# A last stage in which VectorE scales every tile and GpSimd only gathers

## The chip, the cores and the metric

One core of a Trainium2 chip runs the kernel. The time is what the device takes for one execution, in microseconds (us). Three runs of the kernel before gave 1338.32, 1339.25 and 1347.78 us; the median is 1339.25 us.

## The reference

A graph with 10,000 nodes (rows of 512 float32) and 5,000 edges goes through two layers, and each layer ends in a LayerNorm over the 512 columns of a row:

```python
x = _layernorm(x + _L0_gnn_ref(x, W, b, edge_index))      # graph convolution
x = _layernorm(x + _L1_gnn_ref(x, edge_attr, src, dst, ...))  # attention over the edges

# the end of _L1_gnn_ref:
out = segment_sum(m, dst, num_segments=n) ; out = out @ Wo.T + bo
out = node_feat + out
mean = out.mean(axis=0) ; var = jnp.mean(jnp.square(out - mean), axis=0)
out = (out - mean) * rsqrt(var + EPS) * gamma + beta
```

What matters here is the very end. After the attention each node row is `x + u`, where `u` is a message that only nodes with an incoming edge have. A normalisation by column (over all nodes) turns it into `(x + u) * scale + shift`, with one scale and one shift for each of the 512 columns. Then the row `x` is added once more and the LayerNorm by row follows.

## The kernel before

The rows are in 79 tiles of 128 nodes by 512 columns. The stages run one after the other: sorting of the edges, layer 0 over the node tiles, the attention over 20 blocks of 256 edges, and the last stage, `finish_stage`, which all of this case is about. It starts when the sums by column are complete (L2044 and what follows turns them into scale and shift) and then passes over the 79 tiles once. For tile j:

- **ScalarE** copies `x1(j)` (loaded by SyncE's queue, four tiles to a transfer) into the buffer `u(j)` (L2000). There are 12 such buffers; the copy of tile j waits until tile j-12 is summed.
- **GpSimd** then issues an indirect DMA, "the gather" below (L1945), which overwrites those rows of `u(j)` that have a message with their row of `msg_table`. So `u(j)` holds x + u.
- The **scaling** multiplies `u(j)` by the row of scales. For three tiles in four VectorE does it (L2083), reads `u(j)` from SBUF and the scale row from PSUM (`scale = ps[1]`), and writes into one of seven PSUM banks. For tiles with `j % 4 == 2` (`by_pool`) GpSimd does it (L1952) in place in SBUF, with a copy of the scale row in SBUF (`scale_row`), four places behind its gathers (`LATE = 4`).
- **TensorE** adds shift and x1 in the bank: two products for tiles that VectorE scaled (L1992, L1993), three for the others (L1984, L1985, L1987), where the scaled row has to be brought into PSUM too. So that VectorE's own writes can be added to, each bank is first written whole once (`write_whole`, L1956).
- **VectorE** takes the row statistics (`bn_stats`, L2093) and their aggregate (`bn_aggr`, L2100), and for each pair of tiles a reciprocal (L2089) and a bias (L2096); **ScalarE** takes the square root for a pair (L2025) and the normalising pass `y = bank * rstd + bias` (L2030); **SyncE** stores y (L1931, 8 buffers).

The order on each engine is written out by hand, with lags in tiles. VectorE's iteration k is: scaling of k, reciprocal of the pair k-4 (`PAIRED`), statistics of k-2 (`STATS`), bias of that pair, aggregate of k-2. The aggregate waits until the statistics just in front of it are written (`wait_alone`). The scaling of k waits for its gather and until the normalising pass that last read its bank, that of tile k-7, is done (`norm_ok`). ScalarE's iteration k is: copy of k, root of the pair k-12 (in every second iteration), normalising pass of k-15; that pass waits for the pair's bias and until the store that last used its y buffer has landed.

Of the kernel before, what the change touches and what calls it, by code (L numbers as in the profile page):

```python
# [25 lines left out]
ALU = mybir.AluOpType  # L26
# [9 lines left out]
NT = -(-N // P)  # L36
NP = NT * P
ET = -(-E // P)
EP = ET * P
# [15 lines left out]
def wait(eng, sem, count):  # L55

    if isinstance(count, int) and count <= 0:
        return
    eng.wait_ge(sem, count)  # L59


def wait_alone(eng, sem, count, passed):


    eng.wait_ge(sem, count)
    eng.sem_inc(passed, 1)  # L66
# [201 lines left out]
def prologue_stage(nc, g):  # L268
# [6 lines left out]
    PRE = 11  # L275
    LATE = 4
    with ExitStack() as ctx:
# [1547 lines left out]
def finish_stage(nc, g):  # L1825


    sb, sem = g.sb, g.sem
    R = 12
    RY = 8  # L1830
    RM = 8
    AHEAD = 10
    PAIR, NORM = 12, 15
    STATS, PAIRED = 2, 4
    LATE = 4
    with ExitStack() as ctx:
        more = sb(ctx, "fin_x1_more", [P, HOMES - 8, K * D])
        consts = sb(ctx, "fin_consts", [P, 3, K])
        mean = sb(ctx, "fin_mean", [P, K])
        var = sb(ctx, "fin_var", [P, K])  # L1840
        factor = sb(ctx, "fin_factor", [P, 2, K])
        hi = sb(ctx, "fin_factor_hi", [P, 2, K], F32R)
        lo = sb(ctx, "fin_factor_lo", [P, 2, K])
        lo_turned = sb(ctx, "fin_shift_lo_turned", [P, K])
        mirror = sb(ctx, "fin_mirror", [P, P])
        scale_hi = sb(ctx, "fin_scale_hi", [P, K, P], F32R)
        scale_lo = sb(ctx, "fin_scale_lo", [P, K, P], F32R)
        shift_hi = sb(ctx, "fin_shift_hi", [P, K, P])
        shift = sb(ctx, "fin_shift", [P, K, P], F32R)
        ones_r = sb(ctx, "fin_ones", [P, P], F32R)  # L1850
        scale_row = sb(ctx, "fin_scale_row", [P, D])
        stats = sb(ctx, "fin_stats", [P, RM, 6])
        mv = sb(ctx, "fin_mv", [P, RM, 2])
        root = sb(ctx, "fin_root", [P, RM, 1])
        rstd = sb(ctx, "fin_rstd", [P, RM, 1])
        bias = sb(ctx, "fin_bias", [P, RM, 1])
        u_more = sb(ctx, "fin_u_more", [P, K * D])
        ps = g.ps
        g.x1_homes = g.x1_homes + [more[:, i, :] for i in range(HOMES - 8)]
        scale = ps[1]  # L1860
        sum_banks = ps[3:8] + [ps[0], ps[2]]

        def quarter(slot, j):
            return slot[:, j % 4 * D:(j % 4 + 1) * D]

        def x1(j):
            return quarter(g.x1_homes[j // 4 % HOMES], j)

        def u(j):
            return quarter((g.over_lo[:, WK, :], g.over_lo[:, WV, :], u_more)[j // 4 % 3], j)  # L1870

        def y(j):
            return quarter((g.over_lo, g.over_hi)[j // 4 % 2][:, WO, :], j)

        def bank(j):
            return sum_banks[j % 7][:]

        def by_pool(j):
            return j % 4 == 2

        def scaled_by_pool(j):
            return sum(by_pool(i) for i in range(j + 1))

        def scaled_in_psum(j):
            return j + 1 - scaled_by_pool(j)

        const_in = g.const_in
        sums_ok = g.sums_ok
        u_ok, tot_ok, var_ok, std_ok, mirrored = (sem(n) for n in (
            "fin_x_copied", "fin_totals", "fin_var_ok", "fin_std", "fin_mirrored"))  # L1890
        split_ok, rows_ok, wide_ok, shift_ok = (sem(n) for n in (
            "fin_factors_split", "fin_rows_spread", "fin_scale_spread", "fin_shift_ok"))

        u_in = g.sum_in + g.x_in[2:4] + g.part_in + g.x_in[0:2] + g.again_in
        x_in = g.node_in + g.x1_out
        x_before = [landed(NT - 1 - s, 0, 0, 8) for s in range(8)] + [landed(NT - 1 - s, 0, 0, 4) for s in range(4)]
        u_before = [landed(NT - 1 - s, 0, 0, 4) for s in range(4)] + [32 * ET // 4] * 2 + [32 * NB // 2] * 2 + [32 * ET // 4 + 16] * 2 + [16 * (NB - 2)] * 2
        us_ok, pool_ok, sum_ok, stat_ok, root_ok, scale_ok, norm_ok = (sem(n) for n in (
            "fin_u_scaled_in_psum", "fin_u_scaled_by_pool", "fin_y_summed", "fin_stat", "fin_root_ok", "fin_scale_ok", "fin_norm"))
        open_ok = g.open_ok  # L1900
        BANKS = 4 + len(sum_banks)
        SCALE_IN_PSUM, SCALE_ROW = 1, 2
        y_out = g.w_in[1:5] + g.row_out[0:2] + g.u_out
        y_before = [32] * 3 + [16] + [16 * ET // 4] * 2 + [16 * NB] * 2
        mine = g.step_v
# [30 lines left out]
    def gpsimd_program(pool):  # L1936
        pool.wait_ge(g.coef_scanned, K * (NB - 1))
        nc.gpsimd.affine_select(out=mirror[:], in_=g.ones[:], compare_op=ALU.is_equal, fill=0.0, base=1 - P, pattern=[[1, P]], channel_multiplier=1).then_inc(mirrored, 1)
        for out in g.u_out:
            pool.wait_ge(out, 16 * NB)  # L1940

        for k in range(NT + LATE):
            if k < NT:
                pool.wait_ge(u_ok, k + 1)
                nc.gpsimd.indirect_dma_start(out=u(k), out_offset=None, in_=g.msg_table,  # L1945
                                             in_offset=bass.IndirectOffsetOnAxis(ap=g.last_edge[:, k:k + 1], axis=0),
                                             bounds_check=EP - 1, oob_is_err=False).then_inc(u_in[k % R], 16)
            j = k - LATE
            if j >= 0 and by_pool(j):
                pool.wait_ge(wide_ok, SCALE_ROW)  # L1950
                pool.wait_ge(u_in[j % R], u_before[j % R] + 16 * (j // R + 1))
                nc.gpsimd.tensor_tensor(u(j), u(j), scale_row[:], ALU.mult).then_inc(pool_ok, 1)  # L1952

    def tensor_program(pe):
        def write_whole(to):
            pe.matmul(to[:], g.w(g.w_hi, WO, 0, 0, P), g.w(g.w_hi, WO, 0), start=True, stop=True).then_inc(open_ok, 1)  # L1956
# [18 lines left out]
        pe.wait_ge(split_ok, 6)  # L1975
        for whole in sum_banks[5:7]:
            write_whole(whole)
        pe.wait_ge(shift_ok, K)

        for j in range(NT):  # L1980
            if by_pool(j):
                wait(pe, norm_ok, j - 6)
                pe.wait_ge(u_ok, j + 1)
                pe.matmul(bank(j), ones_r[:], shift[:].rearrange("p k n -> p (k n)"), start=True, stop=False)  # L1984
                pe.matmul(bank(j), g.ident[:], x1(j), start=False, stop=False)  # L1985
                pe.wait_ge(pool_ok, scaled_by_pool(j))
                pe.matmul(bank(j), g.ident[:], u(j), start=False, stop=True).then_inc(sum_ok, 1)  # L1987
            else:

                pe.wait_ge(u_ok, j + 1)  # L1990
                pe.wait_ge(us_ok, scaled_in_psum(j))
                pe.matmul(bank(j), ones_r[:], shift[:].rearrange("p k n -> p (k n)"), start=False, stop=False, skip_group_check=True)  # L1992
                pe.matmul(bank(j), g.ident[:], x1(j), start=False, stop=True, skip_group_check=True).then_inc(sum_ok, 1)  # L1993

    def scalar_program(act):
        def copy(j):
# [35 lines left out]
    def vector_program(dve):  # L2032
        v = nc.vector
# [42 lines left out]

        dve.wait_ge(open_ok, BANKS)
        for k in range(NT + PAIRED + 1):
            j = k
            if j < NT and not by_pool(j):  # L2080
                dve.wait_ge(u_in[j % R], u_before[j % R] + 16 * (j // R + 1))
                wait(dve, norm_ok, j - 6)
                v.tensor_tensor(bank(j), u(j), scale[:], ALU.mult).then_inc(us_ok, 1)  # L2083
            done = k - PAIRED
            pair = 0 <= done < NT and (done % 2 == 1 or done == NT - 1)
            m, n = done // 2 * 2 % RM, done % 2 + 1
            if pair:
                dve.wait_ge(root_ok, done // 2 + 1)
                v.reciprocal(rstd[:, m:m + n, :], root[:, m:m + n, :]).then_inc(scale_ok, 1)  # L2089
            j = k - STATS  # L2090
            if 0 <= j < NT:
                dve.wait_ge(sum_ok, j + 1)
                v.bn_stats(stats[:, j % RM, :], bank(j)).then_inc(stat_ok, 1)  # L2093
            if pair:
                dve.wait_ge(scale_ok, done // 2 * 2 + 1)
                v.scalar_tensor_tensor(bias[:, m:m + n, :], mv[:, m:m + n, 0:1], -1.0, rstd[:, m:m + n, :], ALU.mult, ALU.mult).then_inc(scale_ok, 1)  # L2096
            if 0 <= j < NT:
                wait(dve, norm_ok, j - RM + 1)
                wait_alone(dve, stat_ok, 2 * j + 1, g.passed)
                v.bn_aggr(mv[:, j % RM, :], stats[:, j % RM, :]).then_inc(stat_ok, 1)  # L2100

    return sync_program, scalar_program, gpsimd_program, tensor_program, vector_program

# [36 lines left out]
```

## Time and profile before

| | us |
|---|---|
| median of three runs | 1339.25 |
| profiled execution | 1341.85 |
| its span | 1339.9 |
| busy over the span: TensorE / VectorE / ScalarE / GpSimd | 1278.4 / 1081.9 / 636.7 / 815.9 |

The span is the time from the first to the last instruction in the trace; the execution's own time lies 1.95 us above it. The passes of the last stage over its tiles start at 1208.30 us of the span. The rows quoted further down are of three kinds. A row of a timeline is one instruction or a short run of one kind ("x2"): start, duration from the first start to the last end, engine, line, operation, what it writes and reads, and at the end in brackets how long the engine had been idle, and what ended that. The step from one start to the next start on the same engine is what an instruction costs, as durations overlap a little. A row of windows gives the busy time of each engine in one stretch.

### The profile page before, as it was taken

What the parts mean: (1) busy time and instruction counts of PE and PEld (TensorE: products, weight loads), DVE (VectorE), ACT (ScalarE), POOL (GpSimd) and SP (SyncE); (2) the same over time, 40 slices, a digit from 0 to 9 for tenths busy, and PEclk for the clock granted to TensorE, in tenths of its full rate; (3) what the DMA queues carried; (4) which work ended last, traced back from release to release, by engine and by line L of the source; (5) the groups of instructions that cost most, each with busy time, mean ns of one, the idle gap of its engine ahead of it and who ended that gap; (6) DMA issues with size and microseconds to landing.
All of it is one profiled execution on the core that took longest, in us unless ns stands there. A gap on an engine that the chain in (4) does not pass through costs nothing. (4 is left out here: it accounts for less than half of the span.)

```text
span 1339.9 us, 21776 instructions
## 1 busy us (share of the span) xinstructions
PE 1278.4 (95%) x6374; PEld 1028.6 (77%) x6374; DVE 1081.9 (81%) x2035; ACT 636.7 (48%) x1243; POOL 815.9 (61%) x752
## 2 busy tenths in 40 slices
PE   7899999999999699999999999999999999979997
PEld 5778878888888588888888888888888888754332
DVE  7577569999998226888888988888888888888897
ACT  3577547888887212333223323322332333257886
POOL 3667256677675443556666656566666565568885
PEclk9999999999999799999999999999999999879999
DMA  8889768787885514544444344444445443759986
GB/s 282 288 288 309 267 217 274 258 273 260 258 261 172 173 48 111 142 143 137 112 112 131 123 125 130 138 141 130 137 142 142 142 142 95 231 175 385 292 293 222
DMA packets 128300, 257.95 MB, mean 193 GB/s; under 512 B 21459, under 2 KB 21907, under 8 KB 128114
## 3 DMA queue, kind: packets, MB, share of 16 engines
q1 hardware_dynamic: 97490, 175.31, 39.9%
q0 software_dynamic: 29920, 80.38, 20.5%
q10 hardware_dynamic: 832, 1.57, 0.4%
q8 instruction: 26, 0.43, 0.1%
q14 instruction: 32, 0.26, 0.1%
HBM read 197.18 MB, written 73.60 MB: 202 GB/s over the span
## 5 line engine op out<-in xcount | busy, mean ns | idle before, releaser
L208 PE MATMUL ps<-w_lo,w_hi 128*128 128x512 f32 (+2 forms) x1140 | 416.4, 365 | 3.9 <-DVE w_lo L1432 1.4
L210 PE MATMUL ps<-w_hi 128*128 128x512 f32 (+2 forms) x1140 | 410.5, 360 | 0.0
L209 PE MATMUL ps<-w_hi,w_lo 128*128 128x512 f32 (+2 forms) x1140 | 410.4, 360 | 0.0
L208 PEld LDWEIGHTS ps<-w_lo,w_hi 128*128 128x128 f32 x1140 | 217.5, 191 | 36.5 <-DVE w_lo L1514 1.9
L210 PEld LDWEIGHTS ps<-w_hi 128*128 128x128 f32 x1140 | 217.2, 191 | 32.4
L209 PEld LDWEIGHTS ps<-w_hi,w_lo 128*128 128x128 f32 x1140 | 217.6, 191 | 29.6
L1270 POOL TENSOR_TENSOR acc_x<-acc_x,node_rows 128x512 f32<-128x512 f32 x72 | 114.9, 1595 | 86.2 <-DMA node_rows<-x_table 81.9
L925 POOL TENSOR_TENSOR node_y<-node_z,node_x 128x512 f32<-128x512 f32 x79 | 102.6, 1299 | 72.2 <-issue 34.0
L208 PE MATMUL ps<-w_lo,agg_hi 128*128 128x512 f32 x316 | 131.5, 416 | 1.2 <-DVE agg_lo L994 1.2
L209 PE MATMUL ps<-w_hi,agg_lo 128*128 128x512 f32 x316 | 124.8, 395 | 0.0
L210 PE MATMUL ps<-w_hi,agg_hi 128*128 128x512 f32 x316 | 124.7, 395 | 0.0
L1472 DVE TENSOR_TENSOR_SCAN v_turned<-coef_all,carry,v_turned 128x256 f32<-128x256 f32 x76 | 107.7, 1473 | 0.7
L1230 POOL DMA_INDIRECT edge_rows<-x_table,edge_gather_idx x72 | 80.2, 1114 | 42.2 <-POOL edge_gather_idx L1226 28.5
L1361 ACT CAST w_hi<-v_turned 128x1024 fp32r<-128x1024 f32 x17 | 17.9, 1051 | 157.3 <-DVE v_turned L1472 157.3
L1496 DVE TENSOR_TENSOR k_rows<-ps,bk_row 128x512 f32<-128x512 f32 x40 | 27.5, 690 | 73.1 <-PE ps L210 73.1
L929 POOL DMA_INDIRECT node_sum<-sum_table,last_edge x75 | 72.6, 968 | 16.6 <-DVE node_agg L1023 5.2
L1384 ACT ACTIVATE v_turned<-ps,bv_col 128x256 f32<-128x256 f32 x76 | 29.8, 474 | 94.8 <-PE ps L210 94.8
L945 ACT COPY node_z<-ps 128x512 f32<-128x512 f32 x79 | 46.3, 587 | 52.6 <-PE ps L210 52.6
L712 DVE TENSOR_TENSOR_SCAN node_x<-goes_on,node_x,ps 128x128 f32<-128x128 bf16 x156 | 62.0, 462 | 10.6 <-PE ps L624 10.6
L1253 POOL TENSOR_TENSOR k_rows<-k_rows,q_rows 128x512 f32<-128x512 f32 x38 | 49.2, 1296 | 35.0 <-DVE k_rows L1496 34.6
L210 PEld LDWEIGHTS ps<-w_hi,agg_hi 128*128 128x128 f32 x316 | 59.3, 188 | 14.5
L208 PE MATMUL ps<-w_lo,ea_hi 128*128 128x512 f32 x160 | 67.0, 419 | 3.4 <-DVE ea_lo L704 3.4
(279 smaller groups left out, 2866.0 us busy)
## 6 DMA issues: line engine op xcount, KB each, us to landing
node_x<-in_x SPq DMA_DIRECT2D x79, 256.0 KB, 4.1
x_table<-node_x SPq DMA_DIRECT2D x79, 256.0 KB, 2.2
node_rows<-x_table SPq DMA_DIRECT2D x79, 256.0 KB, 8.4
coef_all<-coef_table SPq DMA_DIRECT2D x38, 512.0 KB, 7.3
edge_part<-part SPq DMA_DIRECT2D x40, 256.0 KB, 4.4
out_dram<-rows_over_w_lo SPq DMA_DIRECT2D x40, 256.0 KB, 6.3
node_x<-in_ea SPq DMA_DIRECT2D x38, 256.0 KB, 4.8
msg_table<-dst_rows_and_msg SPq DMA_DIRECT2D x38, 256.0 KB, 5.1
```

Of the source, the lines that this page charges most:

```text
L208: pe.matmul(to, left[0], right[1], start=first, stop=False, skip_group_check=onto)
L209: pe.matmul(to, left[1], right[0], start=False, stop=False, skip_group_check=onto)
L210: return pe.matmul(to, left[0], right[0], start=False, stop=last, skip_group_check=onto)
L712: v.tensor_tensor_scan(run[:, t % R, k, :], g.goes_on[:, t * P:(t + 1) * P], ps_x[t % 2][:, k * P:(k + 1) * P], before, ALU.mult, ALU.add) ...
L925: nc.gpsimd.tensor_tensor(y[:, i % RY, :], z[:, i % 2, :], xr[:, i % RX, :], ALU.add).then_inc(y_ok, 1)
L929: nc.gpsimd.indirect_dma_start(out=rn[:, t % RS, :], out_offset=None, in_=g.sum_table, in_offset=bass.IndirectOffsetOnAxis(ap=g.last_edge[ ...
L945: nc.scalar.copy(z[:, q, :], ps_o[(s - 6) % 4][:]).then_inc(z_ok, 1)
L1230: nc.gpsimd.indirect_dma_start(out=rows[:, q, o, :], out_offset=None, in_=g.x1_table, in_offset=bass.IndirectOffsetOnAxis(ap=at, axis=0)). ...
L1253: nc.gpsimd.tensor_tensor(k_rows[:, q, :], k_rows[:, q, :], q_rows[:, q, :], ALU.mult).then_inc(qk_ok, 1)
L1270: nc.gpsimd.tensor_tensor(g.acc_x[r, :], g.acc_x[r, :], node[r, q, :], ALU.add).then_inc(x_added, 1)
L1384: nc.scalar.activation(vt[:, (s - 1) % 2, m, :], two(ps_r)[m // 2][:, m % 2, :], ACT.Identity, bias=g.bv_col[:, m:m + 1]).then_inc(v_ok, 1)
L1472: v.tensor_tensor_scan(vt[:, s, m, :], coef[:, m, 0, :], vt[:, s, m, :], carry[:, m:m + 1], ALU.mult, ALU.add).then_inc(scan_ok, 1)
```

## The change

VectorE scales all 79 tiles; GpSimd's queue holds the 79 gathers and nothing else. The scale row is read from its copy in SBUF, and the PSUM bank in which it stood becomes the eighth bank for sums (it is written whole as the last one, after ScalarE has copied the row out). TensorE has two products for every tile. VectorE's iteration k is now: statistics of k-3, reciprocal of the pair k-5, scaling of k, bias, aggregate of k-3; the scaling waits for the normalising pass of tile k-8. The core of the diff:

```diff
-    STATS, PAIRED = 2, 4
-    LATE = 4
+    STATS, PAIRED = 3, 5
...
-        sum_banks = ps[3:8] + [ps[0], ps[2]]
+        sum_banks = ps[3:8] + [ps[0], ps[2], scale]
...
-        for k in range(NT + LATE):
-            if k < NT:
-                pool.wait_ge(u_ok, k + 1)
...
-            j = k - LATE
-            if j >= 0 and by_pool(j):
-                pool.wait_ge(wide_ok, SCALE_ROW)
-                pool.wait_ge(u_in[j % R], u_before[j % R] + 16 * (j // R + 1))
-                nc.gpsimd.tensor_tensor(u(j), u(j), scale_row[:], ALU.mult).then_inc(pool_ok, 1)
+        for k in range(NT):
+            pool.wait_ge(u_ok, k + 1)
...
+        pe.wait_ge(wide_ok, SCALE_ROW)
+        write_whole(scale)
         pe.wait_ge(shift_ok, K)
...
-            if by_pool(j):
-                wait(pe, norm_ok, j - 6)
...
+            pe.wait_ge(u_ok, j + 1)
+            pe.wait_ge(us_ok, j + 1)
...
         for k in range(NT + PAIRED + 1):
-            j = k
-            if j < NT and not by_pool(j):
-                dve.wait_ge(u_in[j % R], u_before[j % R] + 16 * (j // R + 1))
-                wait(dve, norm_ok, j - 6)
-                v.tensor_tensor(bank(j), u(j), scale[:], ALU.mult).then_inc(us_ok, 1)
-            done = k - PAIRED
+            stat, done = k - STATS, k - PAIRED
             pair = 0 <= done < NT and (done % 2 == 1 or done == NT - 1)
             m, n = done // 2 * 2 % RM, done % 2 + 1
+            if 0 <= stat < NT:
+                dve.wait_ge(sum_ok, stat + 1)
+                v.bn_stats(stats[:, stat % RM, :], bank(stat)).then_inc(stat_ok, 1)
             if pair:
                 dve.wait_ge(root_ok, done // 2 + 1)
                 v.reciprocal(rstd[:, m:m + n, :], root[:, m:m + n, :]).then_inc(scale_ok, 1)
-            j = k - STATS
-            if 0 <= j < NT:
-                dve.wait_ge(sum_ok, j + 1)
-                v.bn_stats(stats[:, j % RM, :], bank(j)).then_inc(stat_ok, 1)
+            if k < NT:
+                dve.wait_ge(u_in[k % R], u_before[k % R] + 16 * (k // R + 1))
+                wait(dve, norm_ok, k - len(sum_banks) + 1)
+                v.tensor_tensor(bank(k), u(k), scale_row[:], ALU.mult).then_inc(us_ok, 1)
```

Bias and aggregate follow as before, with `stat` in the place of `j`.

## Rows read from the trace of the kernel before

**Rows 1.** Windows: a stretch of 20 us in the last stage, by engine.
```profile
core 0: us, PE busy (x) PEld busy (x) DVE busy (x) ACT busy (x) POOL busy (x), PEclk, DMA share, GB/s
1280.00:1300.00 20.00, 18.30 (x46) 7.87 (x45) 18.07 (x48) 16.17 (x32) 16.54 (x17) 1.00 0.85 274
```

**Rows 2.** Timeline of GpSimd, from one gather to the fourth after it.
```profile
1275.46 0.99 POOL L1945 DMA_INDIRECT rows_over_w_lo<-msg_table,last_edge  x1 [0.31 <-issue]
1276.76 1.00 POOL L1945 DMA_INDIRECT rows_over_w_lo<-msg_table,last_edge  x1 [0.30 <-issue]
...
1279.07 1.29 POOL L1952 TENSOR_TENSOR fin_u_more<-fin_u_more,fin_scale_row 128x512 f32<-128x512 f32 x1
...
1281.86 1.00 POOL L1945 DMA_INDIRECT rows_over_w_lo<-msg_table,last_edge  x1 [0.30 <-issue]
```

**Rows 3.** Timeline of VectorE over the same four tiles.
```profile
1275.31 0.70 DVE L2083 TENSOR_TENSOR ps<-rows_over_w_lo,ps 128x512 f32<-128x512 f32 x1 [0.34 <-DMA rows_over_w_lo<-msg_table,last_edge]
1275.91 0.16 DVE L2089 RECIPROCAL fin_rstd<-fin_root 128x2 f32<-128x2 f32 x1
1275.99 0.68 DVE L2093 BATCH_NORM_STATS2 fin_stats<-ps 128x6 f32<-128x512 f32 x1
1276.59 0.14 DVE L2096 SCALAR_TENSOR_TENSOR fin_bias<-fin_mv,fin_rstd 128x2 f32<-128x2 f32 x1
1276.80 0.18 DVE L2100 BATCH_NORM_AGGREGATE fin_mv<-fin_stats 128x2 f32<-128x6 f32 x1
1276.91 0.69 DVE L2083 TENSOR_TENSOR ps<-fin_u_more,ps 128x512 f32<-128x512 f32 x1
1277.52 0.69 DVE L2093 BATCH_NORM_STATS2 fin_stats<-ps 128x6 f32<-128x512 f32 x1
1278.34 0.18 DVE L2100 BATCH_NORM_AGGREGATE fin_mv<-fin_stats 128x2 f32<-128x6 f32 x1
...
1279.72 0.67 DVE L2096 SCALAR_TENSOR_TENSOR fin_bias<-fin_mv,fin_rstd 128x2 f32<-128x2 f32 x1
...
1281.59 0.70 DVE L2083 TENSOR_TENSOR ps<-fin_u_more,ps 128x512 f32<-128x512 f32 x1 [0.21 <-ACT rows_over_w_lo L2030]
```

**Rows 4.** Timeline of VectorE in the attention stage: operations with two SBUF inputs.
```profile
909.96 3.06 DVE L1579 TENSOR_TENSOR acc_xx<-acc_xx,node_rows 128x512 f32<-128x512 f32 x4
...
1159.67 1.27 DVE L1634 TENSOR_TENSOR k_rows<-k_rows,q_rows 128x512 f32<-128x512 f32 x2
```

**Rows 5.** Timeline where the last stage begins: VectorE, TensorE and the first statistics.
```profile
1206.99 1.22 PE L1956 MATMUL ps<-w_hi 128*128 128x512 f32 x2 [0.26 <-DVE fin_shift_lo_turned L2070]
...
1208.30 1.29 DVE L2083 TENSOR_TENSOR ps<-rows_over_w_lo,ps 128x512 f32<-128x512 f32 x2 [0.19 <-issue]
...
1211.65 0.70 DVE L2093 BATCH_NORM_STATS2 fin_stats<-ps 128x6 f32<-128x512 f32 x1 [2.06 <-PE ps L1993]
```

**Rows 6.** Timeline near the end: the statistics of the last tile.
```profile
1333.77 0.70 DVE L2093 BATCH_NORM_STATS2 fin_stats<-ps 128x6 f32<-128x512 f32 x1 [0.62 <-PE ps L1987]
```

**Rows 7.** Timeline of ScalarE: most of a pair of tiles without a wait.
```profile
1289.71 0.29 ACT L2025 ACTIVATE fin_root<-fin_mv,eps 128x2 f32<-128x2 f32 x1
1289.91 0.76 ACT L2030 ACTIVATE rows_over_w_hi<-ps,fin_bias,fin_rstd 128x512 f32<-128x512 f32 x1
1290.57 0.60 ACT L2000 COPY rows_over_w_lo<-rows_over_w_lo 128x512 f32<-128x512 f32 x1
1291.08 0.78 ACT L2030 ACTIVATE rows_over_w_hi<-ps,fin_bias,fin_rstd 128x512 f32<-128x512 f32 x1
```

**Rows 8.** DMA issues from 1215 to 1335 us (median us to landing last), and L1931.
```profile
rows_over_w_lo<-msg_table,last_edge POOLq DMA_INDIRECT x47, 5.4
...
DMA to landing us min/median/max: 1.6/4.9/9.0
```

**Rows 9.** Timeline at the first gather: a VectorE operation with two SBUF inputs.
```profile
1198.61 0.69 DVE L2044 TENSOR_TENSOR acc_xx<-acc_xx,sum_xx 128x512 f32<-128x512 f32 x1
1198.76 1.48 POOL L1945 DMA_INDIRECT rows_over_w_lo<-msg_table,last_edge  x1 [0.15 <-issue]
```

More of the change, by code:

```diff
@@ L1875, in bank @@
         def bank(j):
[L1876 to L1885, printed above, removed]
+            return sum_banks[j % len(sum_banks)][:]
         const_in = g.const_in
@@ L1897, in finish_stage @@
         u_before = [landed(NT - 1 - s, 0, 0, 4) for s in range(4)] + [32 * ET // 4] * 2 + [32 * NB // 2] * 2 + [32 * ET // 4 + 16] * 2 + [16 * (NB - 2)] * 2
-        us_ok, pool_ok, sum_ok, stat_ok, root_ok, scale_ok, norm_ok = (sem(n) for n in (
-            "fin_u_scaled_in_psum", "fin_u_scaled_by_pool", "fin_y_summed", "fin_stat", "fin_root_ok", "fin_scale_ok", "fin_norm"))
+        us_ok, sum_ok, stat_ok, root_ok, scale_ok, norm_ok = (sem(n) for n in (
+            "fin_u_scaled_in_psum", "fin_y_summed", "fin_stat", "fin_root_ok", "fin_scale_ok", "fin_norm"))
         open_ok = g.open_ok
@@ L1940, in gpsimd_program @@
             pool.wait_ge(out, 16 * NB)
-        for k in range(NT + LATE):
-            if k < NT:
-                pool.wait_ge(u_ok, k + 1)
-                nc.gpsimd.indirect_dma_start(out=u(k), out_offset=None, in_=g.msg_table,
-                                             in_offset=bass.IndirectOffsetOnAxis(ap=g.last_edge[:, k:k + 1], axis=0),
-                                             bounds_check=EP - 1, oob_is_err=False).then_inc(u_in[k % R], 16)
-            j = k - LATE
-            if j >= 0 and by_pool(j):
-                pool.wait_ge(wide_ok, SCALE_ROW)
-                pool.wait_ge(u_in[j % R], u_before[j % R] + 16 * (j // R + 1))
-                nc.gpsimd.tensor_tensor(u(j), u(j), scale_row[:], ALU.mult).then_inc(pool_ok, 1)
+        for k in range(NT):
+            pool.wait_ge(u_ok, k + 1)
+            nc.gpsimd.indirect_dma_start(out=u(k), out_offset=None, in_=g.msg_table,
+                                         in_offset=bass.IndirectOffsetOnAxis(ap=g.last_edge[:, k:k + 1], axis=0),
+                                         bounds_check=EP - 1, oob_is_err=False).then_inc(u_in[k % R], 16)
     def tensor_program(pe):
@@ L1977, in tensor_program @@
             write_whole(whole)
+        pe.wait_ge(wide_ok, SCALE_ROW)
+        write_whole(scale)
         pe.wait_ge(shift_ok, K)
         for j in range(NT):
-            if by_pool(j):
-                wait(pe, norm_ok, j - 6)
[L1983 to L1993, printed above, removed]
+            pe.wait_ge(u_ok, j + 1)
+            pe.wait_ge(us_ok, j + 1)
+            pe.matmul(bank(j), ones_r[:], shift[:].rearrange("p k n -> p (k n)"), start=False, stop=False, skip_group_check=True)
+            pe.matmul(bank(j), g.ident[:], x1(j), start=False, stop=True, skip_group_check=True).then_inc(sum_ok, 1)
     def scalar_program(act):
@@ L2096, in vector_program @@
                 v.scalar_tensor_tensor(bias[:, m:m + n, :], mv[:, m:m + n, 0:1], -1.0, rstd[:, m:m + n, :], ALU.mult, ALU.mult).then_inc(scale_ok, 1)
[L2097 to L2100, printed above, removed]
+            if 0 <= stat < NT:
+                wait(dve, norm_ok, stat - RM + 1)
+                wait_alone(dve, stat_ok, 2 * stat + 1, g.passed)
+                v.bn_aggr(mv[:, stat % RM, :], stats[:, stat % RM, :]).then_inc(stat_ok, 1)
     return sync_program, scalar_program, gpsimd_program, tensor_program, vector_program
```

## The prediction, made before the changed kernel was run

> **What bounds the kernel now.** I read the page first: only the last stage changes, so the row of windows for it comes next. No engine is full there: of 20 us VectorE is busy 18.07, TensorE 18.30, ScalarE 16.17, GpSimd 16.54, at a granted clock of 1.00 and a DMA share of 0.85 [rows 1]. So the timelines have to say who waits. GpSimd's queue does not: a gather starts every 1.30 us (1275.46 to 1276.76; it is busy 1.00 and the other 0.30 is its own issue), and its scaling of 1.29 us stands between two gathers. Four gathers and one scaling take 1281.86 - 1275.46 = 6.40 us, 1.60 us per tile, with no wait for anyone [rows 2]. VectorE covers the same four tiles in 1281.59 - 1275.31 = 6.28 us, with 0.34 us idle for a gather and 0.21 us idle for ScalarE [rows 3]. GpSimd sets the pace, and one place where it passes it on can be seen: the bias, two columns wide, takes 0.14 us at 1276.59 but 0.67 us at 1279.72, and ends at 1280.39, just after GpSimd's scaling, which ran from 1279.07 to 1280.36 [rows 2, 3]. The late aggregate then makes the root, the normalising pass and the next scaling late (the idle 0.21). From the first statistics at 1211.65 to those of the last tile at 1333.77 pass 122.12 us for 78 tiles, 1.57 each [rows 5, 6].
>
> **The change, part by part.** *GpSimd loses its 20 scalings.* Its queue then needs 1.30 us per tile instead of 1.60, and the waits of the bias go with them. It is no longer the bound if another engine needs more than 1.30.
>
> *VectorE gets those 20 scalings and a new order.* I rebuild its iteration from steps. Statistics to the next operation: 0.60 (1275.99 to 1276.59). Scaling to the next: 0.61 (1276.91 to 1277.52). Aggregate to the next: 0.11 (1276.80 to 1276.91). Today the aggregate comes 0.82 us after its statistics (1277.52 to 1278.34), as it must wait for them to be written; with the scaling between them, that wait of some 0.2 us is filled [rows 3]. A tile without pair work costs 0.60 + 0.61 + 0.11 = 1.32. Pair work adds the reciprocal, 0.08 (1275.91 to 1275.99), and the bias; its step to the aggregate, 0.21, is mostly the wait for the statistics, so it lies between 0.08 and 0.21 and I take 0.10, near the reciprocal of the same width. The pair costs 2 x 1.32 + 0.18 = 2.82: **1.41 us per tile**. At 0.21 it would be 1.465.
>
> *The scaling now reads both operands from SBUF.* No row shows this with a result in PSUM. The bounds: the product of two SBUF tiles at L1634 takes 1.27 us for two, a step of 0.60; the sum at L1579 takes 3.06 for four, a step of (3.06 - 0.69) / 3 = 0.79 [rows 4]. I take 0.61: L1579 adds into its own input, so that each waits for the one in front, and the scaling does not. The upper end would make the tile 1.59.
>
> *The eighth bank and the head.* TensorE writes one more bank whole before VectorE may start: half of the 1.22 us of the two written last, 0.61 [rows 5]. VectorE would do three scalings ahead of its first statistics instead of two, but these wait 2.06 us for TensorE today [rows 5], which covers the third (0.61). So the first statistics move to 1211.65 + 0.6 = 1212.25. They stand in iteration 3, so 76 full iterations follow (3 to 78), then two without a scaling before the last statistics: 0.82 + 0.11 each as today, and one pair, 0.18. Last statistics: 1212.25 + 76 x 1.41 + 1.86 + 0.18 = 1321.45, against 1333.77: **12.3 us earlier** [rows 5, 6]. What follows them (6.1 us to the end) has the same operations in the same order.
>
> *ScalarE.* It loses nothing and gains nothing. Root to pass 0.20, pass to copy 0.66, copy to pass 0.51, pass to copy 0.66, and the copy 0.60: 2.63 us per pair, 1.32 per tile [rows 7]. Against 1.41 it has 7% to spare. Its loop with VectorE: the scaling of an even k needs the pass of k-8, which follows the root that needs the aggregate of k-5. Aggregate start, root, end of pass and signal are 0.18 + 0.04 + 0.20 + 0.76 + 0.1, about 1.3 us; from that aggregate to the scaling VectorE has its own work of 0.11 + 1.32 + 0.60 + 0.08 = 2.11. So the wait that is 0.21 today falls away, with 0.8 to spare, thanks to the extra bank and the later place in the iteration.
>
> *TensorE.* It has 20 products fewer; 18.30 busy of 20 us at 12.5 tiles is 1.46 per tile now as the profile models it, but it stood idle for VectorE's scalings, and the statistics now come three iterations (4.2 us) after the scaling. I cost it at nothing. Its cover is the clock of 1.00 [rows 1]; at half of it a tile would cost more than 1.41.
>
> *Gathers and DMA.* A gather lands 5.4 us after its issue [rows 8]. ScalarE copies tile k about nine tiles ahead of VectorE's scaling of k (copy of k stands before the pass of k-15, and the passes follow the scalings by 6 to 7 tiles): 9 x 1.41 = 12.7 us less 1.3 of issue and 5.4 of landing leave 6. The same bytes move in less time: the share goes from 0.85 to 0.85 x 1.57 / 1.41 = 0.95 [rows 1]. The stores land within 9.0 us at most [rows 8], and the pass that reuses a buffer comes 8 x 1.41 = 11.3 us later, less its 0.76 and the issue: 1 us to spare at the worst. This is late next. Price of it: nothing below, up to 0.1 per tile above.
>
> *The lock between VectorE and GpSimd, now the other way round.* The first gather started 0.15 us after a VectorE addition of two SBUF tiles and took 1.48 us instead of 1.00 [rows 2, 9]; it seems to have been held until that addition ended. The new scaling is of that kind and runs 0.6 us of every 1.41. The bounds for a gather are 0 and 0.48. I take it to cost nothing, since a gather that is held leaves at the end of a scaling, and the next one is due 1.30 us later, at the end of the scaling after it: GpSimd falls into step with VectorE at 1.41 and no slower. The Trainium skill says the same of the cause: in "SBUF — State Buffer", section "Who interferes with whom", a VectorE instruction with two SBUF inputs contends with a GpSimd instruction that reads SBUF, and whoever comes first holds the shared port for its whole instruction. By that rule the waits of the bias go, as in the trace, but all 79 scalings now enter the contest, where today none of them does, and the sum would lie between the one above and the third rival below.
>
> **Sum.** 12.3 us off the profiled execution's 1341.85 gives 1329.5; off the median of 1339.25, 2.6 below that execution, it gives **1327.0**. About 1%, 13.4 us, is what a measurement of this kernel can tell from no change; the forecast falls just short of it.
>
> **The rivals.** *First, another engine or the DMA sets the pace* between 1.45 and 1.55: ScalarE waiting for stores, or gathers late under a share of 0.95 [rows 1, 8]. For it: two engines within 7% of VectorE and a DMA that is nearly full. Against it: today ScalarE waits for VectorE, and no DMA but one gather is waited for in these rows. At 1.50 the gain is 12.3 - 76 x 0.09 = 5.5: 1333.8 us.
>
> *Second, the scaling from two SBUF operands costs a step of 0.79* [rows 4], or the exchange does not pay in another way: the gain is 12.3 - 76 x 0.18 = -1.4: about 1340.6 us, no change. Against it: L1634.
>
> *Third, on the other side, the lock decides*: every gather is held by the whole 0.48 [rows 9] and GpSimd's step becomes 1.78, above the 1.60 of today. It decides from a mean hold of 0.30. The last gather would then start at 1198.76 + 1.78 x 78 = 1337.6; landing 5.4, scaling 0.7, TensorE about 1.5 and the 6.1 after the last statistics make a span of 1351.3, 11.4 more than now: 1350.7 us, and more if gathers land later. Against it stands the falling into step, which needs VectorE's regular beat.
>
> **Chances.** Forecast (pace 1.38 to 1.44, 1324.5 to 1329.5): 0.70. First rival (1330 to 1336): 0.15. Second (1337 to 1342): 0.07. Third, with a lower clock of TensorE, whose effect would have the same sign: 0.08. The limit of faster by over 1% is 1325.9. Of the forecast's range a bit over a third lies below it, at paces of 1.39 and less: faster 0.27. Slower by over 1% (above 1352.6) is most of the third case: 0.06. The rest, 0.67, is within 1%. The range of 8 in 10 takes the forecast and most of the first rival: 1324 to 1335 us.
>
> **What would show it.** In the profile after: scalings of VectorE 1.41 us apart on average, an aggregate about 0.6 us after its scaling starts, every bias near 0.14 us, gathers lengthened to at most 1.5 us and in step with VectorE, ScalarE's idle before the root down to about 0.2 us per pair, first statistics near 1212.3, last near 1321.5. Wrong would be: steps of the scaling well above 0.61 (second rival), gathers 1.6 us or more apart with VectorE waiting for DMA (third), a scaling that waits for ScalarE, or stores that land after 10 us (first).

## The result

The changed kernel takes 1323.56 us (median of four runs, 1319.59 to 1327.78), the kernel before 1340.40 (four runs, 1338.32 to 1347.78): the medians are 16.8 us apart. The ratio on record, 0.9858 with a 95% interval of 0.983 to 0.9885, stands for 19.0 us, 1.4% faster. The forecast was 1327.0 with a range of 1324 to 1335 and only 0.27 for faster by over 1%. It missed in size, not in sign.

The first lines of the page after the change (span, busy time by engine):

```profile
span 1317.9 us, 21697 instructions
PE 1265.1 (96%) x6335; PEld 1017.7 (77%) x6335; DVE 1076.7 (82%) x2055; ACT 636.2 (48%) x1243; POOL 790.8 (60%) x732
```

The profiled execution took 1319.59 us, 22.3 less than the one of before (1341.85); its span is 22.0 shorter. Not all of this belongs to the change. Where the last stage begins can be read from an instruction of GpSimd that both kernels have, in code that the change leaves alone. After:

```profile
1194.68 0.28 POOL L1928 TENSOR_SCALAR_AFFINE_SELECT fin_mirror<-ones 128x128 f32<-128x128 f32 x1
...
1208.44 0.70 DVE L2061 BATCH_NORM_STATS2 fin_stats<-ps 128x6 f32<-128x512 f32 x1 [1.45 <-PE ps L1970]
...
1311.72 0.67 DVE L2061 BATCH_NORM_STATS2 fin_stats<-ps 128x6 f32<-128x512 f32 x1
```

Before:

```profile
1198.31 0.30 POOL L1938 TENSOR_SCALAR_AFFINE_SELECT fin_mirror<-ones 128x128 f32<-128x128 f32 x1
```

It came 3.63 us earlier in this execution; over the profiles of this study it lies anywhere from 1194.3 to 1203.5, whatever the kernel. The rest is the stage's own, against [rows 5, 6]:

| stretch | before | after | difference |
|---|---|---|---|
| start to that instruction | 1198.31 | 1194.68 | -3.63 |
| from there to the first statistics | 13.34 | 13.76 | +0.42 |
| first to last statistics (78 tiles) | 122.12 | 103.28 | -18.84 |
| last statistics to the end | 6.13 | 6.18 | +0.05 |

So the stage gained 18.4 us, between the 16.8 of the medians and the 19.0 of the ratio, and all of it in the pace: 1.566 us per tile before, 1.324 after.

Windows of the stage after the change; columns as in [rows 1], whose row this answers:

```profile
1280.00:1300.00 20.00, 19.89 (x47) 7.30 (x45) 20.00 (x61) 19.32 (x38) 15.43 (x15) 1.00 0.98 342
```

VectorE went from 18.07 busy to 20.00 of 20 us: it is full, and ScalarE, at 19.32, nearly so. TensorE stands at 19.89, but its ends are modelled in the profile, and behind the first statistics VectorE waits for it nowhere. GpSimd has fallen from 16.54 to 15.43. The DMA share is 0.98. Timeline of VectorE, a little over two tiles:

```profile
1249.73 0.69 DVE L2061 BATCH_NORM_STATS2 fin_stats<-ps 128x6 f32<-128x512 f32 x1
1250.31 0.17 DVE L2064 RECIPROCAL fin_rstd<-fin_root 128x2 f32<-128x2 f32 x1
1250.38 0.70 DVE L2068 TENSOR_TENSOR ps<-fin_u_more,fin_scale_row 128x512 f32<-128x512 f32 x1
1250.97 0.18 DVE L2071 SCALAR_TENSOR_TENSOR fin_bias<-fin_mv,fin_rstd 128x2 f32<-128x2 f32 x1
1251.04 0.20 DVE L2075 BATCH_NORM_AGGREGATE fin_mv<-fin_stats 128x2 f32<-128x6 f32 x1
1251.13 0.69 DVE L2061 BATCH_NORM_STATS2 fin_stats<-ps 128x6 f32<-128x512 f32 x1
1251.71 0.71 DVE L2068 TENSOR_TENSOR ps<-fin_u_more,fin_scale_row 128x512 f32<-128x512 f32 x1
1252.30 0.20 DVE L2075 BATCH_NORM_AGGREGATE fin_mv<-fin_stats 128x2 f32<-128x6 f32 x1
1252.40 0.69 DVE L2061 BATCH_NORM_STATS2 fin_stats<-ps 128x6 f32<-128x512 f32 x1
```

No row has a bracket: VectorE waits for nobody. A pair of tiles takes 1252.40 - 1249.73 = 2.67 us. Against [rows 3], the 0.82 between statistics and aggregate is gone, and so are the idle 0.34 and 0.21; the bias is 0.18 us long here and 0.28 at most from 1225 to 1305 us, never 0.67. Timeline of GpSimd over the same time:

```profile
1249.70 1.01 POOL L1934 DMA_INDIRECT rows_over_w_lo<-msg_table,last_edge  x1 [0.30 <-issue]
1251.02 1.02 POOL L1934 DMA_INDIRECT rows_over_w_lo<-msg_table,last_edge  x1 [0.30 <-issue]
...
1253.65 1.05 POOL L1934 DMA_INDIRECT fin_u_more<-msg_table,last_edge  x1 [0.30 <-issue]
```

Gathers here follow each other at 1.31 to 1.35 us, where [rows 2] have a scaling between them. From 1249.70 to 1298.92 all of them but one begin 0.60 to 0.65 us behind the start of a scaling and take 1.00 to 1.05 us (the other began 0.37 behind it and took 1.29): GpSimd runs in step with VectorE. The fifth experiment shows what keeps it there. ScalarE, one pair:

```profile
1251.27 0.30 ACT L2002 ACTIVATE fin_root<-fin_mv,eps 128x2 f32<-128x2 f32 x1
1251.47 0.76 ACT L2007 ACTIVATE rows_over_w_hi<-ps,fin_bias,fin_rstd 128x512 f32<-128x512 f32 x1
1252.14 0.61 ACT L1977 COPY fin_u_more<-fin_x_more 128x512 f32<-128x512 f32 x1
1252.64 0.77 ACT L2007 ACTIVATE rows_over_w_hi<-ps,fin_bias,fin_rstd 128x512 f32<-128x512 f32 x1
1253.32 0.61 ACT L1977 COPY fin_u_more<-fin_x_more 128x512 f32<-128x512 f32 x1
1253.93 0.30 ACT L2002 ACTIVATE fin_root<-fin_mv,eps 128x2 f32<-128x2 f32 x1
```

From root to root 1253.93 - 1251.27 = 2.66 us, without a bracket either. It isn't full for all that: the copy in front of the root takes a step of 0.61 and the other one 0.50. In the kernel with half statistics below, where ScalarE hardly waits, both take 0.51 and the pair 2.55.

### The profile page after: what moved, and what is told of

It reads as the page before. It is cut to its first block and busy times, and to the rows that moved or that the text cites. A ratio compares the mean times of both kernels' runs of the same rounds, so it can differ in the third digit from the quotient of the medians.

```text
span 1317.9 us, 21697 instructions
## 1 busy us (share of the span) xinstructions
PE 1265.1 (96%) x6335; PEld 1017.7 (77%) x6335; DVE 1076.7 (82%) x2055; ACT 636.2 (48%) x1243; POOL 790.8 (60%) x732
## 3 DMA queue, kind: packets, MB, share of 16 engines
q10 hardware_dynamic: 832, 1.57, 0.4%
## 5 line engine op out<-in xcount | busy, mean ns | idle before, releaser
L1472 DVE TENSOR_TENSOR_SCAN v_turned<-coef_all,carry,v_turned 128x256 f32<-128x256 f32 x76 | 111.6, 1523 | 0.7
L1348 ACT CAST w_hi<-ps 128x512 fp32r<-128x512 f32 x40 | 21.5, 590 | 100.0 <-PE ps L1714 100.0
```

What stands on the lines that cost most here:

```text
L1472: v.tensor_tensor_scan(vt[:, s, m, :], coef[:, m, 0, :], vt[:, s, m, :], carry[:, m:m + 1], ALU.mult, ALU.add).then_inc(scan_ok, 1)
```

## The experiments

**Which part brings the gain.** Three parts can be taken separately: GpSimd's relief, the new order with its lags, and the eighth bank with the scale row in SBUF. First, the order alone, on the kernel before:

```diff
-    STATS, PAIRED = 2, 4
+    STATS, PAIRED = 3, 5
...
+            if 0 <= stat < NT:
+                v.bn_stats(...)          # ahead of the reciprocal
...
+            if k < NT and not by_pool(k):
+                v.tensor_tensor(bank(k), u(k), scale[:], ALU.mult)   # behind it
```

> The kernel before with the new order alone (statistics of k-3, scaling of k, aggregate of k-3); GpSimd still scales one tile in four, seven banks, scale row in PSUM. If GpSimd's queue (four gathers of 1.30 us and one scaling) sets the pace, the tile stays at 1.57 to 1.60 us and the time within 0.5% of before. If the wait between statistics and aggregate on VectorE was what counted, the pace falls by up to 0.2 us per tile and the time by up to 15 us.

Measured: ratio 1.0024 (1.0004 to 1.0044), 1.64 us per tile. The waits of VectorE from 1225 to 1305 us (total, times, longest):

```profile
DVE ps L2091 <- ACT rows_over_w_lo L2030: 6.8, 13, 0.5
DVE ps L2091 <- ACT rows_over_w_hi L2030: 6.3, 12, 0.9
```

The 0.2 us between statistics and aggregate is filled in the three tiles of four that VectorE scales, and a new wait takes its place: the scaling waits for the normalising pass that frees its bank, 13.1 us in some 49 tiles, 0.27 per tile. With statistics a tile later everything behind them comes a tile later, and seven banks are one too few. The expected pace of 1.57 to 1.60 was for GpSimd's queue as the limit. That limit is still there (four gathers and a scaling, 1.60 per tile [rows 2]), so the order alone could not have gained.

Second, GpSimd's relief alone, on the kernel before:

```diff
-            if j < NT and not by_pool(j):
+            if j < NT:
...
-                nc.gpsimd.tensor_tensor(u(j), u(j), scale_row[:], ALU.mult).then_inc(pool_ok, 1)
```

> The kernel before with VectorE scaling every tile and GpSimd only gathering; old order, seven banks, scale row in PSUM. From the steps of before: scaling 0.60, statistics to aggregate 0.82, aggregate 0.11, reciprocal 0.08 for a pair: 1.57 us per tile, as before; time within 0.5% of before. If GpSimd's relief alone made the gain, the tile takes 1.33 to 1.45 and the time falls by 10 to 19 us.

Measured: ratio 0.9977 (0.9963 to 0.999), 1.567 us per tile. A window of it:

```profile
1250.00:1270.00 20.00, 16.88 (x40) 6.16 (x39) 18.72 (x52) 17.09 (x33) 12.37 (x13) 1.00 0.88 285
```

GpSimd is down to 12.37 of 20 us, so it was relieved, but VectorE in the old order needs 1.57 by itself, the same as before. Two bounds lay one on the other. VectorE's row has 1.28 us of 20 that are not busy, and no DMA or other engine is the cause: they are the aggregate's wait for its own engine's statistics.

Third and fourth, the change with seven banks, the scale row in PSUM as before or in SBUF:

```diff
-        sum_banks = ps[3:8] + [ps[0], ps[2], scale]
+        sum_banks = ps[3:8] + [ps[0], ps[2]]
...
-                v.tensor_tensor(bank(k), u(k), scale_row[:], ALU.mult)
+                v.tensor_tensor(bank(k), u(k), scale[:], ALU.mult)      # p3 only
```

> The changed kernel with seven banks and the scale row in PSUM. The scaling of an odd k then waits for the normalising pass of k-7, which needs the aggregate of k-4 that stands 0.67 us in front of it and 1.29 us are needed: a wait of about 0.6 us per pair, 1.64 us per tile, some 5 us slower than before and 24 slower than the changed kernel. If the eighth bank does not matter: 1.33 and the time of the changed kernel. Theory A (VectorE's steps are 0.02 shorter when its queue is never held up) expects steps of 0.60 behind each wait and 0.58 elsewhere; theory B (the row in SBUF shortens the scaling) expects 0.60 to 0.61 for every scaling here.

> The changed kernel with seven banks, scale row in SBUF. Theory A: the same steps and time as with the row in PSUM (within 1 us). Theory B: scalings 0.02 us shorter than there, some 1.5 us less. If gathers and scalings hold each other up through the shared port, this one is slower than the one with the row in PSUM.

Measured: ratios 1.0017 (0.9998 to 1.0036) and 1.0012 (0.9993 to 1.0032), 1.616 us per tile in both. Where the scale row is read from makes no difference to the pace (0.005 us in the step of a scaling); the eighth bank is the whole difference between these two and the change. VectorE in the version with the row in PSUM:

```profile
1249.37 0.67 DVE L2059 BATCH_NORM_STATS2 fin_stats<-ps 128x6 f32<-128x512 f32 x1
1250.56 0.70 DVE L2066 TENSOR_TENSOR ps<-rows_over_w_lo,ps 128x512 f32<-128x512 f32 x1 [0.52 <-ACT rows_over_w_lo L2005]
1251.16 0.17 DVE L2073 BATCH_NORM_AGGREGATE fin_mv<-fin_stats 128x2 f32<-128x6 f32 x1
...
1251.90 0.68 DVE L2066 TENSOR_TENSOR ps<-rows_over_w_lo,ps 128x512 f32<-128x512 f32 x1
1252.48 0.16 DVE L2069 SCALAR_TENSOR_TENSOR fin_bias<-fin_mv,fin_rstd 128x2 f32<-128x2 f32 x1
```

The scaling at 1250.56 waited 0.52 us for ScalarE and takes a step of 0.60; the next one waited for nothing and takes 0.58. The two stand in different places, but in the change run again, where neither waits, those places differ by 0.005 only. This pair of rows bears on the miss, below.

Fifth, the change with the old order:

```diff
-    STATS, PAIRED = 3, 5
+    STATS, PAIRED = 2, 4
...             # scaling first, then reciprocal, statistics, bias, aggregate, as before
```

> The changed kernel (VectorE scales all, eight banks, scale row in SBUF) with the old order on VectorE: scaling, statistics of k-2, aggregate. If the order is what the gain needs, VectorE's wait between statistics and aggregate stays: 1.567 us per tile, the time of the kernel with VectorE scaling all and seven banks (0.998 of before). If the eighth bank brings the gain by itself: 1.33 to 1.45 per tile, 10 to 19 us below before.

Measured: ratio 1.0003 (0.998 to 1.0025), 1.567 us per tile. VectorE:

```profile
1251.28 0.70 DVE L2060 TENSOR_TENSOR ps<-rows_over_w_lo,fin_scale_row 128x512 f32<-128x512 f32 x1
1251.89 0.69 DVE L2070 BATCH_NORM_STATS2 fin_stats<-ps 128x6 f32<-128x512 f32 x1
1252.72 0.18 DVE L2077 BATCH_NORM_AGGREGATE fin_mv<-fin_stats 128x2 f32<-128x6 f32 x1
```

Statistics to aggregate is 0.83 again. Eight banks do nothing for a kernel that doesn't wait for a bank.

Beside the second experiment, which has the same order but the scale row in PSUM, this kernel also shows how a scaling with two SBUF inputs acts on a gather. A scaling and a gather of the second, then the gather that began 0.27 us behind the scaling at 1251.28 above:

```profile
1248.44 0.69 DVE L2058 TENSOR_TENSOR ps<-rows_over_w_lo,ps 128x512 f32<-128x512 f32 x1
1248.64 1.01 POOL L1934 DMA_INDIRECT rows_over_w_lo<-msg_table,last_edge  x1 [0.31 <-issue]
```

```profile
1251.55 1.30 POOL L1934 DMA_INDIRECT fin_u_more<-msg_table,last_edge  x1 [0.30 <-issue]
```

With the row in PSUM the gather begins 0.20 us behind the scaling and takes 1.01; with both operands in SBUF it takes 1.30. The 40 gathers of this kernel that begin less than 0.56 us behind a scaling's start all end 1.54 to 1.58 us behind that start, whenever they began; the 28 that begin later behind one take 1.00 to 1.01, and so do all 20 of the first kind in the second experiment. So a gather that begins under such a scaling is held until about 0.56 us of the scaling are over. It costs this kernel nothing, since GpSimd has room.

Sixth, the change with GpSimd still scaling one tile in four:

```diff
+            j = k - LATE
+            if j >= 0 and by_pool(j):
+                nc.gpsimd.tensor_tensor(u(j), u(j), scale_row[:], ALU.mult).then_inc(pool_ok, 1)
...
-            if k < NT:
+            if k < NT and not by_pool(k):
```

> New order, eight banks and scale row in SBUF, but GpSimd still scales one tile in four. If GpSimd's queue is a bound of its own, four gathers and one scaling keep the tile at 1.60 us or a little more (scalings of both engines with two SBUF inputs now stand in each other's way): time within 0.5% of before, or up to 8 us slower. If order and bank alone bring the gain: VectorE has three scalings in four, the tile falls to 1.33 or below and the time by 19 us.

Measured: ratio 1.0035 (1.0015 to 1.0056), 1.635 us per tile. VectorE, then GpSimd:

```profile
1249.52 0.66 DVE L2086 BATCH_NORM_STATS2 fin_stats<-ps 128x6 f32<-128x512 f32 x1
1250.10 2.42 DVE L2093 TENSOR_TENSOR ps<-rows_over_w_lo,fin_scale_row 128x512 f32<-128x512 f32 x1
1252.44 0.17 DVE L2100 BATCH_NORM_AGGREGATE fin_mv<-fin_stats 128x2 f32<-128x6 f32 x1
```

```profile
1249.66 1.00 POOL L1945 DMA_INDIRECT rows_over_w_lo<-msg_table,last_edge  x1 [0.30 <-ACT fin_u_more L2002]
1250.67 1.28 POOL L1952 TENSOR_TENSOR rows_over_w_lo<-rows_over_w_lo,fin_scale_row 128x512 f32<-128x512 f32 x1
1252.11 1.31 POOL L1945 DMA_INDIRECT rows_over_w_lo<-msg_table,last_edge  x1 [0.16 <-issue]
```

VectorE's scaling, 0.68 us elsewhere in this trace, takes 2.42 beside GpSimd's, and the gather behind takes 1.31 for 1.00. From 1225 to 1305 us GpSimd scales 12 times, and VectorE's scaling beside it lasts 2.42 to 2.45 us 11 times and 1.57 once; over the stage there are 18 such pairs, and in each VectorE's scaling ends 0.56 to 0.58 us after GpSimd's, whichever began first. With the row in PSUM (the first experiment) none is longer than 0.70; there the bias, whose inputs lie in SBUF too, is the one held (0.39 to 1.56 us). So this is the lock between scaling and scaling, once VectorE reads both operands from SBUF: 1.75 us per four tiles. It isn't what keeps this kernel from gaining, though. GpSimd's queue needs 1.60 per tile without any lock [rows 2], and the lock adds at most 0.07 to that (four tiles take 6.68 us here against 6.40). The parts of the change need each other: leaving out any one of the three (the third to sixth experiments) loses the gain, and no subset tried gained more than 0.3%.

**What the miss hangs on.** The change once more, and with the scaling first in the iteration again but the aggregate one tile later, so that it never waits for statistics just in front of it:

```diff
+            j = k                        # scaling of k, first in the iteration
...
+            j = k - 2                    # statistics of k-2
...
+            j = k - STATS                # aggregate of k-3, on a semaphore of its own
+                wait_alone(dve, stat_ok, j + 1, g.passed)
+                v.bn_aggr(mv[:, j % RM, :], stats[:, j % RM, :]).then_inc(aggr_ok, 1)
```

> The changed kernel with the scaling first again (scaling of k, reciprocal, statistics of k-2, bias), but with the aggregate one tile later (k-3), so that it never waits for the statistics in front of it. If what the new order saves is that wait, and VectorE's steps are 0.02 us shorter when nothing holds it up: steps of 0.58 to 0.59, 1.33 us per tile, the time of the changed kernel (0.986 of before). The scaling now stands 0.67 us earlier against ScalarE's pass, with some 0.1 us to spare, so that a few waits may make it 1.35. If the place of the scaling between statistics and aggregate matters in itself: 1.45 to 1.57.

> The changed kernel once more, beside the other two. 1.33 us per tile with every step as in its first trace (0.58 statistics, 0.59 scaling, 0.09 aggregate, 0.07 reciprocal and bias), whatever the stages ahead of it take; time 0.986 of before, within 0.002.

Measured: 0.9848 (0.9831 to 0.9864) and 0.9861 (0.984 to 0.9883), 1.334 and 1.333 us per tile. VectorE with the late aggregate:

```profile
1251.87 0.67 DVE L2061 TENSOR_TENSOR ps<-rows_over_w_lo,fin_scale_row 128x512 f32<-128x512 f32 x1
1252.45 0.69 DVE L2071 BATCH_NORM_STATS2 fin_stats<-ps 128x6 f32<-128x512 f32 x1
1253.05 0.17 DVE L2079 BATCH_NORM_AGGREGATE fin_mv<-fin_stats 128x2 f32<-128x6 f32 x1
1253.13 0.68 DVE L2061 TENSOR_TENSOR ps<-fin_u_more,fin_scale_row 128x512 f32<-128x512 f32 x1
```

Against the fifth experiment only the aggregate's place differs. Its hold is gone (0.83 to 0.60), and the step of the scaling went with it from 0.61 to 0.58, that of the aggregate from 0.11 to 0.08. The step of the statistics did not: with nothing held it is 0.60 (1252.45 to 1253.05), not the 0.58 to 0.59 that was expected. It is as fast as the change; the intervals overlap, so it doesn't beat it.

**What sets the pace now.** Each kernel halves the work of one engine per tile: the statistics, ScalarE's pass (from tile 8), both.

```diff
-                v.bn_stats(stats[:, stat % RM, :], bank(stat))
+                v.bn_stats(stats[:, stat % RM, :], bank(stat)[:, 0:D // 2])          # q1, q3
...
-                nc.scalar.activation(y(j), bank(j), ACT.Identity, ...)
+                w = D if j < RY else D // 2
+                nc.scalar.activation(y(j)[:, 0:w], bank(j)[:, 0:w], ACT.Identity, ...)   # q2, q3
```

> The changed kernel with row statistics over 256 of the 512 columns (left out: the other half), which takes 0.27 us per tile off VectorE (1.33 to 1.06). If ScalarE, whose pair takes 2.66 us as well, is a second bound: the pace stays at 1.33 and VectorE shows idle time behind ScalarE or GpSimd. If VectorE alone is the bound: 1.31, where GpSimd's gathers (1.30 to 1.31) stop it.

> The changed kernel with the normalising pass of ScalarE over 256 of the 512 columns from tile 8 on (left out: the other half of y), which takes 0.43 us per pair off ScalarE (2.66 to 2.23). If VectorE is a bound of its own: the pace stays at 1.33 and ScalarE idles 0.4 us per pair before the root. If only ScalarE was: 1.31.

> The changed kernel with row statistics and, from tile 8 on, the normalising pass over 256 of the 512 columns (left out: the other halves). VectorE needs 1.06 us per tile, ScalarE about 1.08. If GpSimd's gathers are the third bound: 1.31 us per tile as soon as their lead is used up, and VectorE waits for gathers. If the DMA (share 1.0) is: more than 1.31, with gathers or stores late.

Measured: ratios 0.984 (0.978 to 0.9899), 0.9858 (0.9798 to 0.9918) and 0.9847 (0.9827 to 0.9866); paces over the stage 1.284, 1.335 and 1.302. One window of each, in this order:

```profile
1250.00:1270.00 20.00, 19.67 (x48) 7.42 (x47) 18.27 (x64) 20.00 (x41) 15.43 (x16) 1.00 1.04 368
```

```profile
1250.00:1270.00 20.00, 19.87 (x46) 7.26 (x46) 20.00 (x62) 16.43 (x38) 15.43 (x16) 1.00 1.02 354
```

```profile
1230.00:1250.00 20.00, 17.73 (x47) 8.21 (x48) 17.04 (x64) 17.92 (x42) 15.73 (x15) 1.00 1.06 400
```

With a lighter ScalarE (16.43) nothing moves: VectorE stays at 20.00, so ScalarE's 19.3 to 19.9 of 20 was no second bound. With lighter statistics the pace improves by 0.04 to 0.05 only, then ScalarE is at 20.00. That pace is below the 1.31 expected from GpSimd's gathers, whose step is 1.345 there: they start 10 us ahead of the first scaling, and the stage ends before this lead is used up. With both lighter neither is full, and VectorE waits for gathers to land (total, times, longest, from 1208 to 1300 us):

```profile
DVE ps L2069 <- DMA rows_over_w_lo<-msg_table,last_edge: 9.4, 10, 3.4
```

One of its gathers, and the scaling under which it began:

```profile
1280.80 0.68 DVE L2069 TENSOR_TENSOR ps<-rows_over_w_lo,fin_scale_row 128x512 f32<-128x512 f32 x1
1280.96 1.40 POOL L1934 DMA_INDIRECT fin_u_more<-msg_table,last_edge  x1 [0.30 <-issue]
```

GpSimd is never idle here for more than the 0.30 of its own issue. Its gathers take 1.10 us on average, by the same hold as in the fifth experiment, and follow each other at 1.40 from the first to the last, while they land 6.2 us after their issue against 6.0 with half the pass alone (medians, rows_over_w_lo). So behind VectorE's 1.33 stand ScalarE at 1.28 and, with both out of the way, late gathers, mainly because GpSimd's full queue issues them at 1.40. Stores were late as well: ScalarE waited 2.8 us for two of them. That GpSimd's queue would be the bound in a longer stage is an estimate from these steps; no experiment took the holds away alone. Each pace of this group is that of one trace, and the times of the three can't be told from the change's. The DMA share alone doesn't tell whether gathers come late: the second of the three kernels had a window with nearly the same share and rate and VectorE full:

```profile
1230.00:1250.00 20.00, 19.84 (x46) 7.24 (x46) 20.00 (x60) 16.88 (x39) 15.43 (x16) 1.00 1.06 395
```

## Why the prediction was wrong

**The bound before: right, but half of it.** GpSimd at 1.60 per tile and the held bias [rows 2, 3] were as described; from first gather to last it made 1.59 per tile (the last began at 1322.95), and the stage ran at 1.57 out of the lead of its gathers. Taking GpSimd's scalings away alone gave 0.2%, since VectorE's old order, given all scalings, needs 1.567. The prediction had all three remedies in one sum, so this didn't hurt it.

**GpSimd's relief: right.** Its step is 1.31 (forecast 1.30), busy 15.43 of 20.

**The filled wait: right.** The aggregate starts 0.59 after its scaling (forecast 0.6) and waits for nothing.

**The eighth bank and ScalarE's loop: right.** No scaling waits for a bank; with seven banks each tile would lose 0.27 to 0.29. ScalarE had 4% to spare where 7% had been expected, because VectorE is faster than forecast. Its own need was put too high as well: the sum of 2.63 takes the last copy by its duration, 0.60, and not by its step, 0.51 [rows 7]; 2.55 was measured, 1.28 per tile.

**First statistics: right.** +0.42 from the stage's start (forecast +0.6). **The tail: right**, 6.18.

**The scaling's operands: right.** The row in SBUF or PSUM gave the same pace, 1.616. The second rival (a step of 0.79) did not occur.

**TensorE and the stores at nothing: right.** The clock granted is 1.00 in the window, nothing waited for TensorE once the stage ran, and ScalarE waited for two stores, 0.6 us in total. The latest store landed after 10.3 us (before 9.0), which the prediction had named as a sign of the first rival; the sign came without the slowdown.

**The lock with the gathers at nothing: right, and by the mechanism forecast.** A gather that begins under a scaling with two SBUF inputs is held until some 0.56 us of it are over (fifth experiment); the first gather of [rows 9] ended 1.63 us behind its addition's start, a little later than the 1.54 to 1.58 there. In the change GpSimd falls into step behind the scalings, as forecast, and the gathers take 1.03 us on average: a mean hold of 0.03, far from the 0.30 of the third rival, and below the 0.11 that would have put GpSimd's 1.30 above the forecast's 1.41. The lock between scaling and scaling cost VectorE 1.75 us per four tiles in the sixth experiment. The Trainium skill ("SBUF — State Buffer", section "Who interferes with whom") names this pair as contending, and the sixth experiment agrees. It also lets the first comer hold the port for its whole instruction; here VectorE's scaling began 0.57 us before GpSimd's and was the one lengthened, while GpSimd's kept its 1.28. The measurement decides: the one that starts first in the trace is not always the one that wins. The spans of GpSimd are rough in a profile, so when each engine asked for the port stays open.

**VectorE's pair: this step failed.** The prediction put it at 2 x (0.60 + 0.61 + 0.11) + 0.08 + 0.10 = 2.82 us, 1.41 per tile. Measured: 2 x (0.58 + 0.59 + 0.09) + 0.07 + 0.07 = 2.66, 1.33 per tile. Over 76 iterations that is 76 x 0.08 = 6.1 us; the forecast 12.3 and 6.1 make the 18.4 that the stage gained. The mechanism was right and its largest term mis-sized, by 0.02 or so in each instruction.

The difference of 0.16 per pair, from steps averaged over 80 us, is 0.04 in the two scalings, 0.04 in the two statistics, 0.04 in the two aggregates and 0.04 in reciprocal and bias. Where do they come from? The steps of [rows 3] were read in a queue that is held up once in every tile, by the aggregate's wait for the statistics in front of it. For the scaling and the aggregate this is the difference that counts. A scaling takes 0.60 to 0.61 behind a held aggregate (before, the second and fifth experiments) or when it has itself waited (the first, third and fourth), and 0.58 to 0.59 otherwise in these kernels and the change, whether it stands first or second in the iteration, and with the second operand in PSUM or SBUF. The late aggregate, against the fifth experiment, moves nothing else and shows both steps shrink.

The statistics do not follow this rule. They take 0.58 directly behind an aggregate, in the change and also in the first, third, fourth and sixth experiments, where other instructions are held. Behind a reciprocal they take 0.59 to 0.60 in the kernels with that hold, and the same with the late aggregate, which has none (0.60 behind the scaling there). So their share goes with the place that the new order gives them and not with the hold. Why an instruction after a hold takes longer to the next, and why the neighbour matters to the statistics, is not shown by any run.

The rows had a hint. The prediction bounded the scaling's step by L1634, "1.27 us for two, a step of 0.60" [rows 4]; less the 0.69 that it used for the other row of the group, this gives 0.58, the measured value. (The next operation starts 1.20 us behind the first of the two, so 0.60 is the mean of that step and of the one to the next operation.) The bias had bounds on both sides, 0.08 and 0.21; the scaling's lower end was that 0.60, and statistics and aggregate had no range at all. The bias came out at 0.07, below its lower bound.

**The chances.** The forecast lay 1 us from the limit of 1%, and its range ended 0.44 us above the measured median. That distance is less than the four runs differ among themselves, so on which side of 1324 the median fell was chance; the stage's own 18.4 us against 12.3 were not. There is also a slip in the working: of the forecast's range, 1324.5 to 1329.5, 1.4 of 5.0 us lie below 1325.9, 0.28 and not "a bit over a third", which makes 0.20 of the 0.27. With a bound from below on the steps (0.58 for the scaling, the same for the statistics of equal width, the reciprocal's 0.08 for the bias) the pair is 2 x (0.58 + 0.58 + 0.11) + 0.16 = 2.70 us and the gain 76 x 0.06 = 4.6 more, 1322.4: the range would have had to reach down to it, and "faster" deserved about half of the chance.

## What to carry to other kernels

When a sum is built from steps of one engine, take them from a stretch in which the engine isn't held up and the instruction has the neighbours that it will have, or give every term a bound from below as well: 0.02 us in 0.60, 76 times over a few instructions, was a third of the gain. Where an instruction waits for the one in front of it, work of another tile put between them fills the wait, but the deeper pipeline wants one more buffer; test both together, as each without the other showed nothing here. When two bounds coincide, neither remedy alone tells you anything about the pair.

## What the runs showed of the hardware

- VectorE's step for a scaling of 512 float32 columns is 0.58 to 0.59 us, and 0.60 to 0.61 after a hold; for statistics it is 0.58 behind an aggregate and 0.59 to 0.60 behind a scaling or a reciprocal. The change run again gives the same in another execution, 2.66 us for a pair:

```profile
1249.24 0.66 DVE L2061 BATCH_NORM_STATS2 fin_stats<-ps 128x6 f32<-128x512 f32 x1
...
1251.90 0.66 DVE L2061 BATCH_NORM_STATS2 fin_stats<-ps 128x6 f32<-128x512 f32 x1
```

- A scaling of VectorE with two SBUF inputs beside GpSimd's product takes 2.42 us for 0.68 and ends 0.56 to 0.58 us after it (18 of 18). Gathers do not lengthen it (0.81 at most, in a stretch of the change where every VectorE row reads some 0.1 us longer at unchanged steps).
- It does lengthen a gather that begins under it: 40 of 40 in the fifth experiment ended 1.54 to 1.58 us behind the scaling's start, against 1.00 to 1.01 us of their own. With one input in PSUM none of 20 was lengthened (second experiment).
- A DMA share of 1.06 at 395 GB/s went with a full VectorE in one kernel, and 1.06 at 400 GB/s with late gathers in another that asks for them faster. A high share is by itself no sign of a wait here.
- The unchanged part ahead of the stage ends anywhere within 9 us from one execution to the next. Effects of a few us have to be read from the stage's own rows, or from several rounds.
